# One program block for the opening: feed-forward of batch 0 ahead of the query-weight folding, output weights folded by pairs among the down tiles

## The chip, the cores and the metric

The kernel runs on one core of one Trainium2 chip. The time is the device time of one execution in microseconds (us). The engines are named PE (TensorE), DVE (VectorE), ACT (ScalarE), POOL (GpSimd) and SP (SyncE); ACT and SP also issue the DMA transfers.

## The reference

Four batches of 512 rows of 512 numbers pass a half-weighted feed-forward, a latent attention with 32 heads, and the feed-forward again. All of it is float32.

```python
x = x + 0.5 * ffn(layernorm(x))
x = x + attn(layernorm(x))
x = x + 0.5 * ffn(layernorm(x))

# ffn: W_base 512x512, four active LoRA experts of rank 8, gates from a softmax
y = x @ W_base.T + b_base
alpha = softmax(log(prior + EPS) + x @ router_W.T + router_b)
return y + einsum(lora_B @ (lora_A @ x) * 2, alpha)

# attn
c_q, c_kv, k_rope = x @ w_q_down, x @ w_kv_down, rope(x @ w_k_rope)
q_lat = einsum(c_q @ w_q_up_nope, w_uk)          # w_q_up_nope (192 x 4096), w_uk (4096 x 64)
q_rope = rope(c_q @ w_q_up_rope)
probs = softmax(causal((q_lat . c_kv + q_rope . k_rope) / sqrt(192)))
out = einsum(probs @ c_kv, w_uv) @ w_out          # w_uv (4096 x 64), w_out (4096 x 512)
```

## The kernel before

The weights are prepared once, then the four batches run one after the other. A weight that multiplies in float32 precision is kept as a high part (written by ACT) and a low part (the rest, written by DVE or POOL).

The first program block prepares weights. PE transposes W_base (`wb_hi`, `wb_lo`). It then folds w_uk into w_q_up_nope in eight groups of four heads: `transpose_nope` turns a group into two banks, ACT and DVE copy them out, and `fold_query` multiplies them with `uk_sb`. Behind the first two groups ACT and DVE also split the rotary weights (`rotary_hi`, `rotary_lo`). Last come the LoRA weights, the gate's prior and the down weights (`wd_hi` on ACT, `wd_lo` on POOL). All engines meet at the end of this block.

The second block starts with `steps(-1, FIRST, STEPS)` for batch 0. Its tiles 4 to 7 are the feed-forward of the four row tiles and its tiles 8 to 11 the down projections. For each tile PE does a first half of the products, a transpose for the tile before (`transpose_z` or `transpose_down`), the transpose of the next tile's normalised rows (`transpose_x`), one `fold_output`, the second half, and for a feed-forward tile the LoRA product of the tile before (`lora`). In the opening the tiles alternate over two pairs of PSUM banks, so a tile's first half waits until `update_rows` on DVE has emptied the pair two tiles before. `fold_output` folds w_uv into w_out, four heads at a time, from two staging buffers that SP fills (`load_out`); a buffer is loaded again when PE has used it. POOL computes rough inverse deviations, which DVE refines. After tile 11 come the first query products of batch 0, and then the attention loop.

Each engine runs its own instructions strictly in the written order; semaphores tie the engines together. SP's and ACT's transfers go to one queue each, served in order.

## Time and profile before

| | us |
|---|---|
| median of 3 runs | 1360.4 (1359.52 to 1362.66) |
| the profiled execution, its own time | 1361.4 |
| its span, first to last instruction | 1359.5 |
| PE busy | 1212.1 (89%) |
| DVE busy | 851.1 (63%) |
| ACT busy | 629.7 (46%) |
| POOL busy | 512.1 (38%) |

The busy shares are means over the whole span, of which nine tenths are attention and later feed-forwards that the change doesn't touch. What the change moves lies in the first 128.5 us, so the rows further down are from there. In a timeline row the first number is the start, the second the length from the first to the last of the merged instructions, and the bracket gives idle time ahead of it and who ended it.

### The profile page before, as it was taken

The page shows a single profiled execution, that of the slowest core. Times are in us where ns is not written, and L with a number is a line of the kernel's source. Part 1 is how long each engine was busy: PE and PEld are TensorE (multiplying, and loading weights), DVE is VectorE, ACT ScalarE, POOL GpSimd, SP SyncE. Part 2 cuts the span into 40 slices and gives each one's busy share as a digit, 9 for nine tenths or more (in the row PEclk, how much of TensorE's full clock was granted, in tenths as well). Part 3 has the DMA queues.
Part 4 walks back from the last instruction along what each step waited for, and adds up shares of the span by engine and source line. Part 5 has one row for each costly group of instructions (what it writes and reads, how often), then busy time and mean ns, then how long its engine had stood idle before and what let it go on. Part 6 is the DMA issues. An engine that isn't in the chain of part 4 may idle for free.

```text
span 1359.5 us, 27786 instructions
## 1 busy us (share of the span) xinstructions
PE 1212.1 (89%) x8424; PEld 1014.2 (75%) x8424; DVE 851.1 (63%) x3266; ACT 629.7 (46%) x1810; POOL 512.1 (38%) x821
## 2 busy tenths in 40 slices
PE   3587899999988799999989699999989789999997
PEld 3465788888777678888769578888869678888876
DVE  1564666666667566566667565666666566665655
ACT  1433655555413455555512455555532365555541
POOL 0311544444312344444421254444430254444430
PEclk8799999999989899999989899999998899999998
DMA  9251000000000000000000000000010000000000
GB/s 263 85 169 40 1 1 1 0 0 2 32 24 10 3 2 1 0 0 1 2 32 32 3 1 1 0 0 1 1 32 32 1 1 1 1 0 0 2 1 31
DMA packets 21232, 27.64 MB, mean 20 GB/s; under 512 B 9942, under 2 KB 11734, under 8 KB 20474
## 3 DMA queue, kind: packets, MB, share of 16 engines
q1 hardware_dynamic: 16922, 17.98, 4.2%
q10 hardware_dynamic: 4192, 8.19, 2.1%
q8 instruction: 62, 1.02, 0.3%
q14 instruction: 56, 0.46, 0.1%
HBM read 21.97 MB, written 4.19 MB: 19 GB/s over the span
## 4 chain that ended last, share of the span: by engine, by line
issue 36%; POOL 27%; PE 24%; DVE 6%; ACT 1%; POOLq 1%; DVEq 0%; ACTq 0%
POOL prob L701 20%; POOL q_tok L674 6%; PE Y L747 5%; PE Y L932 4%; PE XZ L747 3%; PE Y L906 3%; PE XZ L891 2%; PE XZ L720 1%; PE Y L793 1%; PE Y L840 1%; DVE x_sb L1301 1%; DVE stats L1106 1%; PE XZ L870 1%; PE Y L852 1%; PE XZ L872 1%
## 5 line engine op out<-in xcount | busy, mean ns | idle before, releaser
L701 POOL TENSOR_TENSOR prob<-prob,small 128x512 f32<-128x512 f32 (+3 forms) x512 | 360.6, 720 | 462.6 <-DVE small L1297 461.7
L1078 ACT ACTIVATE prob<-XZ,small 128x512 f32<-128x512 f32 (+3 forms) x512 | 266.7, 525 | 351.4 <-DVE small L1342 351.3
L1342 DVE CUSTOM_DVE_ANT_0 XZ<-XZ,mask 128x512 f32<-128x512 f32 (+3 forms) x512 | 244.4, 508 | 254.3 <-issue 245.4
L870 PE MATMUL XZ<-kT_hi,qT_hi 128*128 128x512 f32 (+3 forms) x512 | 181.8, 355 | 25.0 <-DVE qT_lo L1290 14.9
L891 PE MATMUL XZ<-ident,prob 128*128 128x128 f32 x1280 | 195.5, 275 | 0.2
L872 PE MATMUL XZ<-kT_hi,qT_lo 128*128 128x512 f32 (+3 forms) x512 | 166.1, 324 | 0.0
L871 PE MATMUL XZ<-kT_lo,qT_hi 128*128 128x512 f32 (+3 forms) x512 | 165.8, 324 | 0.0
L891 PEld LDWEIGHTS XZ<-ident,prob 128*128 128x128 f32 x1280 | 147.5, 140 | 21.1 <-POOL prob L701 7.3
L906 PE MATMUL Y<-probT,ckv 128*64 128x384 f32 (+2 forms) x1280 | 152.3, 384 | 8.6 <-ACT probT L596 8.1
L596 ACT ACTIVATE probT<-XZ 128x512 f32<-128x512 f32 x192 | 114.6, 597 | 79.5 <-PE XZ L891 77.2
L906 PEld LDWEIGHTS Y<-probT,ckv 128*64 128x64 f32 x1280 | 84.1, 136 | 71.2 <-issue 44.0
L674 POOL TENSOR_TENSOR q_tok<-q_tok,q_sin 128x256 f32<-128x256 f32 x128 | 93.2, 728 | 110.3 <-DVE q_sin L1282 105.6
L870 PEld LDWEIGHTS XZ<-kT_hi,qT_hi 128*128 128x128 f32 x512 | 97.3, 190 | 47.8 <-issue 40.7
L1301 DVE TENSOR_TENSOR x_sb<-Y,x_sb 128x512 f32<-128x512 f32 x128 | 87.9, 686 | 70.5 <-PE Y L932 70.2
L932 PE MATMUL Y<-wo_hi,oT_hi 128*128 128x512 f32 (+1 forms) x256 | 111.3, 435 | 1.6 <-DVE x_sb L1301 1.4
L852 PE MATMUL Y<-ident,q_tok 128*128 128x128 f32 x512 | 81.7, 283 | 30.4 <-POOL q_tok L674 30.4
L872 PEld LDWEIGHTS XZ<-kT_hi,qT_lo 128*128 128x128 f32 x512 | 97.2, 190 | 5.8
L932 PE MATMUL Y<-wo_hi,oT_lo 128*128 128x512 f32 (+1 forms) x256 | 100.9, 394 | 0.0
L1078 ACT ACTIVATION_READ_ACCUMULATOR prob<-XZ,small 128x1 f32 x512 | 100.3, 196 | 0.0
L932 PE MATMUL Y<-wo_lo,oT_hi 128*128 128x512 f32 (+1 forms) x256 | 100.0, 391 | 0.0
L871 PEld LDWEIGHTS XZ<-kT_lo,qT_hi 128*128 128x128 f32 x512 | 98.0, 191 | 2.2
L1290 DVE TENSOR_TENSOR qT_lo<-Y,qT_hi 128x512 fp32r<-128x512 f32 x128 | 86.1, 672 | 12.1 <-ACT qT_hi L1047 12.1
(203 smaller groups left out, 2500.3 us busy)
## 6 DMA issues: line engine op xcount, KB each, us to landing
wout_nat<-in_L_attn_w_out_dram SPq DMA_DIRECT2D x8, 1024.0 KB, 5.7
out_dram<-x_sb SPq DMA_DIRECT2D x16, 256.0 KB, 2.0
x_next<-_attn_hidden_states_dram SPq DMA_DIRECT2D x12, 256.0 KB, 2.9
nope_a<-_L_attn_w_q_up_nope_dram ACTq DMA_DIRECT2D x2, 1024.0 KB, 14.5
wbase_nat<-in_L_ffn_W_base_dram ACTq DMA_DIRECT2D x1, 1024.0 KB, 5.5
nope_b<-_L_attn_w_q_up_nope_dram ACTq DMA_DIRECT2D x2, 512.0 KB, 13.3
rope_a<-_L_attn_w_q_up_rope_dram ACTq DMA_DIRECT2D x1, 1024.0 KB, 11.1
rope_bb<-_L_attn_w_q_up_rope_dram ACTq DMA_DIRECT2D x2, 512.0 KB, 13.4
```

The costliest lines, as they stand in the source:

```text
L596: do.activation(probT_unit(v), bank_unit(v), ACT.Copy).then_inc(probT_by_act, 1)
L674: nc.gpsimd.tensor_tensor(rot, rot, q_sin[:, :, ::-1, :], ALU.add).then_inc(q_tok_set, 1)
L701: last = nc.gpsimd.tensor_tensor(prob[u % RING][:, c:c + w], prob[u % RING][:, c:c + w], inv_sum[:, u % RING, m:m + 1].broadcast_to([P, w] ...
L747: last = nc.tensor.matmul(banks_of(s, first(b + 1))[:, half, 0:z - a], xt[s % 2][:, c, :], w[:, c, a:z], start=(c == 0 and j == 0), stop=( ...
L870: nc.tensor.matmul(bank[:, c:c + w], high, kT_hi[:, 0:w], start=True, stop=False)
L871: nc.tensor.matmul(bank[:, c:c + w], high, kT_lo[:, 0:w], start=False, stop=False)
L872: last = nc.tensor.matmul(bank[:, c:c + w], low, kT_hi[:, 0:w], start=False, stop=True)
L891: last = nc.tensor.transpose(probT_ps[v % 2][:, at], prob[v % RING][:, at], ident[:])
L906: last = nc.tensor.matmul(o_ps[64 * h:64 * h + 64, column * P:(column + n) * P], ckv[:, j, :], probT[:, HEAD_BLOCKS * h + at:HEAD_BLOCKS * ...
L932: last = nc.tensor.matmul(bank, o[buffer][:, rows], w, start=(k == 0 and j == 0), stop=(k == 1 and j == 2))
L1078: last = nc.scalar.activation(prob[u % RING][:, c:c + w], score_ps[u % 2][:, c:c + w], ACT.Exp, bias=neg_max[:, u % RING, m:m + 1], scale= ...
L1342: last = nc.vector.tensor_tensor_reduce(bank, bank, mask[:, S - w:S], -1.0, HIGHEST, ALU.add, ALU.min, neg_max[:, u % RING, m:m + 1])
```

## The change

The two program blocks become one, and the opening of every engine is written out by hand.

- ACT issues W_base, then the four row tiles of x (before: SP, behind the small gathers), then w_uk; the first half of w_q_up_nope follows only after the W_base splits. The second half, the rotary weights and the down weights move to SP.
- On SP the LoRA gathers of all four experts go first, the eight small gate gathers (router bias, prior) after them.
- DVE takes the statistics of x among the W_base splits, so tile 4 can be normalised and multiplied before any query weight is folded.
- Order on PE: W_base, tile 4's transpose, LoRA weights, feed-forward tiles 4 to 7, the query folding (with the rotary weights as before), then the down tiles 8 to 11.
- The statistics of the four down tiles are taken together after the last feed-forward tile, and POOL computes their rough deviations in one group, behind `wd_lo`.
- The first two staging buffers of the output weights are loaded without a wait. `fold_output` now takes two heads and one PSUM bank of three (16 folds for 8). Two folds stand ahead of tile 8, then three to a tile, five behind and in tile 11.
- Later batches keep their order; only counts of semaphores change there.

```diff
+        outw_banks = (Y[0][:, 0, :], Y[0][:, 1, :], Z[0])
+        FOLDS_FIRST = (0, 1)
+        FOLDS = {8: ((2,), (3, 4)), 9: ((5,), (6, 7)), 10: ((8,), (9, 10)), 11: ((11,), (12, 13, 14, 15))}
@@ SP: the reload of a staging buffer
-                            sp.wait_ge(outw_ps, g - 1)
+                            sp.wait_ge(outw_ps, 2 * (g - 1))
@@ ACT
+                def opening():
+                    act.dma_start(wbase_nat[:], W_base.rearrange("(c p) h -> p c h", p=P)).then_inc(ffn_in, 16)
+                    for t in range(ST):
+                        act.dma_start(x_sb[:, t, :], hidden[0, t * P:(t + 1) * P, :]).then_inc(x_in[t], 16)
+                    act.dma_start(uk_sb[:], w_uk.rearrange("(h d) r -> d h r", d=DN)).then_inc(uk_in, 16)
+                    for c in range(KC):
+                        base_high(c)
...
@@ POOL
+                    z_constants()
+                    rough_deviations(0, FIRST, ST)
+                    pool.wait_ge(down_hi_set, 1)
+                    nc.gpsimd.tensor_tensor(wd_lo[:], down_nat[:], f32(wd_hi[:]), ALU.subtract).then_inc(down_lo_set, 1)
+                    rough_deviations(1, DOWN, ST)
+                    pool.wait_ge(rope_hi_set, 1)
...
@@ PE
+                def fold_output(i):
+
+                    j, at = (i // 2) % 2, 2 * (i % 2)
+                    pe.wait_ge(out_in[j], 32 * (i // 4 + 1))
+                    if i >= 3:
+                        pe.wait_ge(outw_hi, i - 2)
+                        pe.wait_ge(outw_lo, i - 2)
+                    bank = outw_banks[i % 3]
+                    for h in range(2):
+                        last = nc.tensor.matmul(bank[64 * h:64 * h + 64, :], uv_nat[j][:, at + h, :],
+                                                wout_nat[j][:, at + h, :], start=True, stop=True, tile_position=(0, 64 * h))
+                    last.then_inc(outw_ps, 1)
+                def opening():
+                    transpose_base()
+                    transpose_x(-1, FIRST)
+                    transpose_lora()
+                    pe.wait_ge(lora_lo_set, 1)
+                    for s in range(FIRST, DOWN):
...
+                        ffn_products(-1, s, 0)
...
+                    pe.wait_ge(nope_in[0], 32)
+                    transpose_nope(0, 0)
+                    transpose_z(-1, DOWN - 1)
+                    lora(-1, DOWN - 1)
...
+                    for i in range(G4 // 2):
+                        fold_query(i)
+
+                    transpose_x(-1, DOWN)
+                    for i in FOLDS_FIRST:
+                        fold_output(i)
...
+                        down_products(-1, s, 0)
+                        if s > DOWN:
+                            transpose_down(-1, s - 1)
+                        if s + 1 < STEPS:
+                            transpose_x(-1, s + 1)
+                        for i in FOLDS[s][0]:
+                            fold_output(i)
+                        down_products(-1, s, 1)
+                        for i in FOLDS[s][1]:
+                            fold_output(i)
@@ DVE
+                def opening():
+                    nc.vector.memset(f32(cq_lo[64:P, 1, :]), 0.0)
+                    base_low(0)
+                    base_low(1)
+                    for t in range(ST):
+                        dve.wait_ge(x_in[t], 16)
+                        nc.vector.bn_stats(stats[:, t, :], x_sb[:, t, :]).then_inc(stats_set, 1)
+                    base_low(2)
+                    base_low(3)
...
+                    nopeTb_copy(0, 0)
+                    z_low(-1, DOWN - 1)
+                    update_rows(-1, DOWN - 1)
+                    for s in range(DOWN, STEPS):
+                        dve.wait_ge(x_updated, s - DOWN + 1)
+                        row_stats(-1, s)
+                    dve.wait_ge(stats_set, 2 * ST)
+                    for s in range(DOWN, STEPS):
+                        last = row_moments(s)
+                    last.then_inc(var_set, 1)
+                    deviations(1, DOWN, ST, 2)
+                    norm(-1, DOWN, FIRST)
+                    norm(-1, DOWN + 1, FIRST)
+                    pipelined(dve, query_lo, rotary_lo)
```

The order of instructions shows the change at three places. First, what ACT issues at the program's start, before:

```order
L324 DMA wbase_nat<-in_L_ffn_W_base_dram 128x4x512
L325 DMA uk_sb<-in_L_attn_w_uk_dram 128x32x64
L333 DMA nope_a<-in_L_attn_w_q_up_nope_dram 128x2048
L335 DMA nope_b<-in_L_attn_w_q_up_nope_dram 64x2048
L328 DMA rope_a<-in_L_attn_w_q_up_rope_dram 128x2048
L330 DMA rope_bb<-in_L_attn_w_q_up_rope_dram 64x2048 x2
L333 DMA nope_a<-in_L_attn_w_q_up_nope_dram 128x2048
L335 DMA nope_b<-in_L_attn_w_q_up_nope_dram 64x2048
L341 ACT_TABLE_LOAD
L341 ACTIVATE wb_hi<-XZ 128x256
```

and ACT at the same place of the changed program:

```order
L1004 DMA wbase_nat<-in_L_ffn_W_base_dram 128x4x512
L1006 DMA x_sb<-in_L_attn_hidden_states_dram 128x512 x4
L1007 DMA uk_sb<-in_L_attn_w_uk_dram 128x32x64
L967 ACT_TABLE_LOAD
L967 ACTIVATE wb_hi<-XZ 128x256
```

The first W_base split now stands behind six issues instead of nine, and none of them is a query weight; the two of `nope_a` and `nope_b` that ACT keeps stand behind its eighth activation.

Second, DVE between the last weight work and the first normalised tile of the next stage; before, this is the seam of the two blocks, ahead of the feed-forward:

```order
L501 TENSOR_TENSOR small<-small,router_row 128x4
L278 UNCONDITIONAL_BRANCH
L1094 UNCONDITIONAL_BRANCH
L1110 BN_AGGR moments<-stats 128x2 x4
L1117 TENSOR_TENSOR newton<-rough 128x4
```

and in the changed program the same kind of work stands between the last feed-forward tile and the query folding (`nopeT_b` is the first operand copy of a query group that PE waits for):

```order
L1205 SCALAR_TENSOR_TENSOR x_sb<-XZ,x_sb 128x512
L1134 BN_STATS stats<-x_sb 128x6 x4
L1138 BN_AGGR moments<-stats 128x2 x4
L1145 TENSOR_TENSOR newton<-rough 128x4
L1147 TENSOR_TENSOR newton<-newton,var_eps 128x4
L1149 TENSOR_SCALAR newton<-newton 128x4
L1151 TENSOR_TENSOR rstd<-newton,rough 128x4
L1157 TENSOR_SCALAR xn_79<-x_sb,moments,rstd 128x512
L1157 TENSOR_SCALAR xn_80<-x_sb,moments,rstd 128x512
L1252 COPY nopeT_b_75<-XZ 128x256
L1262 TENSOR_TENSOR wq_lo<-Y,wq_hi 128x4x64
L1265 TENSOR_TENSOR wq_56<-Y,wq_56 64x4x64
```

The copy for the second query group is now queued behind the statistics, the deviations and two normalised tiles.

Third, PE in the third down tile (tile 10), from the transpose of the tile before it to the end of its second half; before:

```order
L782 MATMUL XZ<-ident,down_101 128x128 x3
L720 MATMUL XZ<-ident,xn_89 128x128 x4
L793 MATMUL Y<-wout_nat_128,uv_nat_126 64x512 x4
L756 MATMUL Y<-wd_hi,xT_hi_90 128x320
L756 MATMUL Y<-wd_lo,xT_hi_90 128x320
L756 MATMUL Y<-wd_hi,xT_lo_92 128x320
L756 MATMUL Y<-wd_hi,xT_hi_90 128x320
L756 MATMUL Y<-wd_lo,xT_hi_90 128x320
L756 MATMUL Y<-wd_hi,xT_lo_92 128x320
```

and in the changed program:

```order
L617 MATMUL XZ<-ident,down_92 128x128 x3
L561 MATMUL XZ<-ident,xn_80 128x128 x4
L687 MATMUL XZ<-wout_nat_128,uv_nat_126 64x512 x2
L591 MATMUL Y<-wd_hi,xT_hi_81 128x320
L591 MATMUL Y<-wd_lo,xT_hi_81 128x320
L591 MATMUL Y<-wd_hi,xT_lo_83 128x320
L591 MATMUL Y<-wd_hi,xT_hi_81 128x320
L591 MATMUL Y<-wd_lo,xT_hi_81 128x320
L591 MATMUL Y<-wd_hi,xT_lo_83 128x320
L687 MATMUL Y<-wout_nat_128,uv_nat_126 64x512 x2
L687 MATMUL Y<-wout_nat_129,uv_nat_127 64x512 x2
```

A tile held one fold of four heads; it now holds three folds of two, and the third needs the other staging buffer.

## Rows read from the trace of the kernel before

**Rows 1.** Stretches: length, busy PE, PEld, DVE, ACT, POOL (counts), clock, DMA share, GB/s

```profile
0.00:51.00 51.00, 25.31 (x339) 21.30 (x340) 15.06 (x32) 16.59 (x35) 8.64 (x14) 0.87 0.66 185
51.00:64.90 13.90, 2.03 (x13) 1.31 (x11) 8.92 (x25) 5.35 (x9) 5.63 (x9) 0.61 0.44 123
64.90:118.80 53.90, 46.58 (x266) 31.77 (x267) 29.28 (x78) 18.27 (x43) 6.75 (x28) 0.94 0.47 144
```

**Rows 2.** Timeline of PE: W_base, first query groups, first feed-forward product

```profile
6.42 1.08 PE L393 MATMUL XZ<-ident,wbase_nat 128*128 128x128 f32 x4 [6.42 <-DMA wbase_nat<-in_L_ffn_W_base_dram]
...
28.03 0.48 PE L423 MATMUL XZ<-uk_sb,nopeT_a 128*64 128x64 f32 x4 [7.34 <-ACT nopeT_a L359]
...
31.60 0.48 PE L423 MATMUL Y<-uk_sb,nopeT_a 128*64 128x64 f32 x4
...
40.73 0.48 PE L423 MATMUL Y<-uk_sb,nopeT_a 128*64 128x64 f32 x4 [4.11 <-issue]
...
64.88 0.58 PE L747 MATMUL Y<-wb_hi,xT_hi 128*128 128x292 f32 x1 [1.50 <-DVE xT_lo L1136]
```

**Rows 3.** Timeline of ACT: a blocked issue and the first W_base split

```profile
2.35 6.65 ACTq L333 DMA_DIRECT2D nope_a<-_L_attn_w_q_up_nope_dram  x1
...
14.25 0.38 ACT L341 ACTIVATE wb_hi<-XZ 128x256 fp32r<-128x256 f32 x1
```

**Rows 4.** Timeline of DVE: W_base's last split, statistics, moments, first normalised tile, row update

```profile
18.86 0.41 DVE L455 TENSOR_TENSOR wb_lo<-Y,wb_hi 128x256 fp32r<-128x256 f32 x1
...
52.99 2.47 DVE L491 BATCH_NORM_STATS2 stats<-x_sb 128x6 f32<-128x512 f32 x4
...
58.64 0.38 DVE L1110 BATCH_NORM_AGGREGATE moments<-stats 128x2 f32<-128x6 f32 x4 [1.17 <-PEq L278]
...
61.47 1.19 DVE L1129 TENSOR_SCALAR xn<-x_sb,moments,rstd 128x512 f32<-128x512 f32 x2
...
85.49 0.68 DVE L1177 SCALAR_TENSOR_TENSOR x_sb<-XZ,x_sb 128x512 f32<-128x512 f32 x1
```

**Rows 5.** DMA queues from 12 to 16 us (q10 ACT's, q1 SP's): packets, MB

```profile
q10 hardware_dynamic: 176, 1.30, 98.8%
q1 hardware_dynamic: 172, 0.02, 3.9%
```

**Rows 6.** Timeline of PE: an output fold, and the first halves of tiles 5 to 7

```profile
68.38 1.94 PE L793 MATMUL Y<-wout_nat,uv_nat 128*64 128x512 f32 x8
...
71.77 0.30 PE L747 MATMUL XZ<-wb_hi,xT_hi 128*128 128x292 f32 x1
...
78.95 0.40 PE L747 MATMUL Y<-wb_hi,xT_hi 128*128 128x292 f32 x1 [0.89 <-DVE x_sb L1177]
...
86.23 0.41 PE L747 MATMUL XZ<-wb_hi,xT_hi 128*128 128x292 f32 x1 [0.89 <-DVE x_sb L1177]
```

**Rows 7.** Timeline of PE in tiles 9 to 11: two waits, a fold, one half tile

```profile
100.58 0.41 PE L756 MATMUL XZ<-wd_hi,xT_hi 128*128 128x320 f32 x1 [1.96 <-DVE x_sb L1177]
...
102.90 3.09 PE L793 MATMUL Y<-wout_nat,uv_nat 128*64 128x512 f32 x8
...
112.07 0.41 PE L756 MATMUL Y<-wd_hi,xT_hi 128*128 128x320 f32 x1
...
113.05 0.31 PE L756 MATMUL XZ<-wd_hi,xT_hi 128*128 128x320 f32 x1
...
115.44 0.55 PE L782 MATMUL Y<-ident,down 128*128 128x128 f32 x3 [1.35 <-ACT ckv L1000]
```

**Rows 8.** SP's issue of the third output load; landing of all eight

```profile
71.09 0.38 SPq L625 DMA_DIRECT2D wout_nat<-in_L_attn_w_out_dram  x1
...
DMA to landing us min/median/max: 5.0/5.7/7.9
```

**Rows 9.** Timeline of PE: first query products and first scores

```profile
118.76 0.28 PE L840 MATMUL Y<-wq_hi,cq_hi 128*128 128x256 f32 x1
...
128.54 0.47 PE L870 MATMUL XZ<-kT_hi,qT_hi 128*128 128x512 f32 x1 [1.50 <-DVE qT_lo L1290]
```

More of the change, by code:

```diff
@@ L260, in rounds, with pipelined @@
                 body(i)
-        def pipelined(eng, opening, body, between):
-            opening()
+        def pipelined(eng, body, between):
             body(0)
@@ L683, in steps @@
                     z_constants()
-                    if start == 0:
-                        rough_deviations(group + (2 if end > FIRST else 1), 2, 2)
+                    rough_deviations(group + (2 if end > FIRST else 1), 2, 2)
                     if end > DOWN:
@@ L797, in steps, with transpose_base @@
-                def steps(b, start, end):
-                    transpose_x(b, start)
-                    for s in range(start, end):
+                def transpose_base():
+                    pe.wait_ge(ident_set, 3)
+                    pe.wait_ge(ffn_in, 16)
+                    for c in range(KC):
+                        if c >= 2:
+                            pe.wait_ge(base_hi, c - 1)
+                            pe.wait_ge(base_lo, c - 1)
+                        for o in range(KC):
+                            last = nc.tensor.transpose(weights_ps[c % 2][:, o * P:(o + 1) * P],
+                                                       wbase_nat[:, o, c * P:(c + 1) * P], ident[:])
+                        last.then_inc(baseT_ps, 1)
@@ new lines, in transpose_lora @@
+                def transpose_lora():
+                    pe.wait_ge(lora_in, 16 * (3 * NE + 1))
+                    pe.wait_ge(base_lo, KC)
+                    for c in range(KC):
+                        last = nc.tensor.transpose(weights_ps[1][:, c * (NZ + NE):(c + 1) * (NZ + NE)],
+                                                   lora_nat[:, c * P:(c + 1) * P], ident[0:NZ + NE, 0:NZ + NE])
+                    last.then_inc(loraT_ps, 1)
+                    pe.wait_ge(up_filled, 1)
+                    for o in range(KC):
+                        last = nc.tensor.transpose(weights_ps[0][:, o * P:(o + 1) * P], up_nat[:, o, :], ident[:])
+                    last.then_inc(upT_ps, 1)
@@ new lines, in transpose_nope @@
+                def transpose_nope(g, j):
+                    for h in range(4):
+                        nc.tensor.transpose(nopeTa_ps[j][:, h * P:(h + 1) * P],
+                                            nope_a[:, 4 * g + h, :], ident[:])
+                    for h in range(4):
+                        last = nc.tensor.transpose(nopeTb_ps[j][:, h * 64:(h + 1) * 64],
+                                                   nope_b[:, 4 * g + h, :],
+                                                   ident[0:64, 0:64])
+                    last.then_inc(nopeT_ps, 1)
@@ L801, in steps @@
+                def steps(b, end):
+                    transpose_x(b, 0)
+                    for s in range(end):
                         products = ffn_products if s < DOWN else down_products
-                        wait_for_products(b, s, start)
+                        wait_for_products(b, s)
                         products(b, s, 0)
-                        if s > start:
+                        if s:
                             (transpose_z if s <= DOWN else transpose_down)(b, s - 1)
@@ L1018, in steps @@
+                def steps(b, end):
+                    xT_high(b, 0)
+                    for s in range(end):
+                        if s:
                             (z_high if s <= DOWN else ckT_high)(b, s - 1)
@@ new lines, in steps @@
+                def steps(b, end):
+                    group, roughs = 2 + 3 * b, GROUPS_0 + GROUPS * b
+                    norm(b, 0)
+                    norm(b, 1)
+                    dve.wait_ge(y_added, 32 * (b + 1))
+                    for t in (2, 3):
+                        row_stats(b, t)
+                    xT_low(b, 0, 12 * b + 8 + (2 * ST if end > FIRST else ST))
+                    row_moments(2)
+                    row_moments(3).then_inc(var_set, 1)
+                    if end > FIRST:
+                        deviations(group + 1, FIRST, ST, roughs + 1)
+                        deviations(group + 2, 2, 2, roughs + 3)
+                    else:
+                        deviations(group + 1, 2, 2, roughs + 2)
+                    for s in range(end):
+                        if 0 <= s - 2 < DOWN:
```

675 lines of the change are left out of this document (343 added, 332 removed).

## The prediction

> **What bounds the kernel now.** I read the page first: PE is busy in 89% of the span, but that mean says nothing of the opening. So I split the first 128.5 us by what PE works on [rows 1]. The reader is to see four stretches. The first 51 us prepare weights, with PE busy for 25.3 of them. Then come 13.9 us in which PE is busy for 2.03: the last weights, the seam of the two blocks, and the norm of the first tile. The feed-forward, the down tiles and the output folds take 53.9 us with PE busy for 46.6. The first queries take 9.8 (118.76 to 128.54) [rows 9]. Everything after 128.5 us keeps its order, so what the change is worth is the start of batch 0's scores, 128.54 us now [rows 9], against where they start afterwards.
>
> Next the timelines of each engine, to see who is late. Three things hold up the first stretch. ACT's DMA issue of `nope_a` blocks for 6.65 us, so the first W_base split starts at 14.25 [rows 3] although the transposes it needs ran from 6.42 to 7.50 [rows 2]. The query folding starts at 28.03 after PE waited 7.34 us. And it stops for 4.11 us in the middle, for the rotary weights [rows 2]. During all this x isn't used at all. The third stretch is close to PE's own work, so there the sum is one of PE time plus waits.
>
> **The change part by part.** I write the new opening as a chain on the clock of the profile.
>
> *Start to first product.* Nothing blocks ACT any more, so the splits start at 7.5. From their start to the last low part took 5.0 us (14.25 to 19.27) [rows 3, 4]. The statistics of x, 2.47 us [rows 4], are put between; W_base's 1 MB had landed at 6.42 [rows 2], so x, the next MB on the same queue, should be there near 10.2 (estimate), and part of the 2.47 fits in DVE's gaps. I take 14.1 for the end. From moments to the first norm is 2.83 us (58.64 to 61.47) [rows 4], from there to the first product 3.41 (61.47 to 64.88) [rows 2, 4]: 20.3. The LoRA gathers may be later than that. In 12 to 16 us the two queues moved 172 and 176 packets [rows 5], one for one, so SP's small packets pass at the rate of ACT's large ones while `nope_a` and `nope_b` stream, here 1.5 MB or some 5 us. I add 0.9: first product at 21.2. The gate's own gathers come last, but the gate is used only behind the first half tile, and I count nothing for them; if that cover were gone, it would be the same few us as in the rival below.
>
> *Feed-forward.* The first half of tile 4 runs at 64.88, of tile 5 at 71.77, of 6 at 78.95, of 7 at 86.23 [rows 2, 6]. Each period holds one output fold of 1.94 us that now moves away: 4.95, 5.24 and 5.34 remain. The waits of 0.89 us for `update_rows` stay, since DVE's 0.68 us starts right when PE's LoRA product ends [rows 4, 6]. In the first period DVE's low part of the next tile loses its cover, which was the fold; I add 0.35. Tile 7's first half then starts at 37.1. What is left of it (two halves, one LoRA product, without another transpose) I take as 3.7, and 2.9 for the first query transposes, the wait for DVE and the last LoRA product: 43.7. These two are estimates, the periods above less the transpose and the wait.
>
> *The new wait.* Here a stall comes back. DVE's copy for the second query group is queued behind the last row update, four statistics, moments to norm, and two norms: 0.68 + 2.47 + 2.83 + 1.19 [rows 4], with the copy itself of about 0.4 and starts 7.7. PE can do one group of folding, then it waits some 4.5 us. The second group starts at 51.4. POOL's `wd_lo` runs beside DVE's statistics, ends about with them and costs nothing more; if it were late, each us would be one of the total. From the second group to the end took 19.2 us (31.60 to 50.8) [rows 1, 2], with its stop for the rotary weights and a slow clock at its start, and both come again: 70.7. The seam of the blocks itself is gone, and 13.9 us have become these 4.5.
>
> *Down tiles and output folds.* One transpose and two folds: 2.5, so tile 8 starts at 73.2. PE's work from there is eight half tiles of 0.98 (112.07 to 113.05) [rows 7], fourteen folds of 0.95, a little under half of 1.94 [rows 6], and the transposes, for which I take 2.7 together (estimate): 23.8 us. Now the loads. A buffer is free when a pair of folds has ended, and from the end of a fold to the landing is 0.77 us until the issue (70.32 to 71.09) and 5.0 to 5.7 of transfer [rows 6, 8]; 6.1 together. With two folds and the two buffers loaded ahead, the chain is: fold 1 ends at 73.2, fold 4 can start at 79.3; 4.5 us of work bring fold 5 to its end, fold 8 can start 6.1 after that; 2.9 us bring fold 9 to its end, fold 12 can start 6.1 after that; then fold 11's own reload holds fold 14, and two folds follow. That is 30.9 us from tile 8 to the last fold, 7.1 more than PE's work: 104.1. What is late is always the load, since the folds of 1.1 MB used to be 7.3 us apart and now are nearer.
>
> *First queries.* 9.8 us as before [rows 9], of which I take 0.3 off, because the last down tile's copies are done long before: 113.6.
>
> *Clock.* After 1.96 us of idle, the longest in the down tiles, the fold took 3.09 us [rows 7] for 1.94, as at 1.2 GHz; after the three of 0.89 and the two of 1.35 it stayed fast (two and one of them stand in [rows 6, 7]). The new waits are of 1 to 2.4 us. I count one such fall, 0.45 on the transpose and 1.15 on the fold: 1.6, so 115.2.
>
> The sum: 128.5 less 115.2 is 13.3 us. The profiled execution took 1361.4 with its span of 1359.5, which gives 1348.1; it lies 1 us above the median of 1360.4, and against that the forecast is 1347.1.
>
> A rule speaks against this change more than my one fall does. The Trainium skill, TensorE: Matmul & The Clock Gate, section "HAM oscillation — how this bites in real kernels", says that a kernel whose short bursts of matmuls alternate with DMA waits starts every burst at the low clock. The trace shows one fall in six such waits, after 1.96 us and not after 0.89 or 1.35, so I hold to one.
>
> **The rivals.**
>
> *Every load wait drops the clock.* Four waits at 1.6 us each is 6.4 for the 1.6 in the sum: 1351.9. For it speaks the fall after 1.96 us, against it that no shorter wait did it. The rule just named gives this time.
>
> *The loads are slower.* Two are in flight at once, and the pair that was issued together took up to 7.9 us [rows 8]. That is 2.6 more in three rounds: 7.8, so 1354.9. For it speaks that new loads follow each other every 5 us; against it that 1.1 MB in 5 us is 220 GB/s, while the stretch moved 144 with pauses [rows 1].
>
> *The loads hide.* If a reload lands while PE does other things, because the tiles before are slower than I think, the 7.1 and the 1.6 fall away: 1338.4.
>
> *The small gathers are late.* If SP's packets go one for one behind large ones throughout [rows 5], the first product comes 5 us later: 1352.1. Against it: ACT's queue holds only half of `nope` then.
>
> *Slower than before.* PE's clock stays at 1.2 GHz from the wait at 45 us to the scores. A query group took 3.57 us at that level (28.03 to 31.60) [rows 2] and 19.2 for seven is 2.7 on average, so 6 us more; the down stretch at 3.09 for 1.94 [rows 6, 7] is 14 more of which the load waits absorb about 3. With 17 us lost it is 1364. It decides from 13.3 us lost, that is, a low clock for some three quarters of 51 to 104 us. Against it, 0.94 was granted in the whole third stretch, with PE busy for 86% of it [rows 1]; after, it is 75 to 80%.
>
> **How the numbers follow.** The forecast with its own spread (1343 to 1351) has 0.50. Each load wait dropping the clock 0.10, slower loads 0.10, late gathers 0.10, hidden loads 0.13; slower than before 0.03. The other 0.04 is that waits which I haven't seen eat most of it. The range goes from the hidden loads to the slower loads, 1338 to 1355.5, and leaves about 0.12 out. A measurement here tells apart 0.2%, 2.7 us. All cases but the last two gain more: faster 0.94, same 0.03, slower 0.03.
>
> **What would show it.** In the new profile: the first W_base split near 7.5; the first feed-forward product near 21; three periods near 5.3 with DVE ending a wait of 0.9 in each; a wait of PE of 4 to 5 us for DVE's `nopeT_b` before the second query group, near 51; the folding's end near 71; waits of 1 to 2.4 us ahead of folds 4, 8, 12 and 14; the first scores at 113 to 116; and from there to the end the same 1231 us. The forecast is wrong if SP's gathers hold up DVE ahead of the first low part, if `wd_lo` on POOL ends after DVE's moments, or if the granted clock is low in the down tiles.

## The result, and the profile after

The changed kernel takes 1347.7 us (median of 4 runs, 1345.4 to 1348.5) where the kernel before, run beside it, took 1361.5. The ratio is 0.990, with a 95% interval of 0.988 to 0.992: 1.0% faster. The profiled execution has a span of 1346.4 us.

First the windows of PE's stretches, as in [rows 1], cut where the changed program changes its work (columns as there). They are: weights, feed-forward, query folding, down tiles, first queries.

```profile
0.00:19.20 19.20, 6.61 (x28) 4.93 (x28) 8.96 (x29) 4.94 (x12) 4.77 (x21) 1.00 0.88 253
19.20:42.30 23.10, 20.07 (x136) 19.08 (x137) 11.37 (x40) 8.95 (x21) 0.00 (x0) 1.00 0.98 276
42.30:68.90 26.60, 19.25 (x315) 16.46 (x313) 16.00 (x37) 12.24 (x24) 10.75 (x4) 0.81 0.06 22
68.90:105.50 36.60, 29.43 (x138) 13.56 (x137) 18.43 (x45) 15.74 (x39) 0.00 (x0) 0.95 0.62 194
105.50:115.20 9.70, 4.84 (x33) 3.78 (x31) 5.12 (x15) 3.01 (x7) 1.45 (x2) 0.88 0.00 0
```

The reader is to see where PE rests: 12.6 us of the first 19.2, then 3.0 in the feed-forward, 7.4 in the folding and 7.2 in the down tiles. The scores start at 115.24 for 128.54 [rows 9], and from there to the end it is 1231.2 us for 1231.0. So the gain of the profiled execution, 13.3 us, lies wholly in the first part.

The timeline of PE gives the stations of that chain and the waits ahead of them (its other waits are left out):

```profile
19.20 0.61 PE L582 MATMUL Y<-wb_hi,xT_hi 128*128 128x292 f32 x1
...
20.10 0.45 PE L582 MATMUL Y<-wb_hi,xT_hi 128*128 128x292 f32 x1
...
25.63 0.38 PE L582 MATMUL XZ<-wb_hi,xT_hi 128*128 128x292 f32 x1 [0.43 <-DVE xT_lo L1164]
...
30.70 0.40 PE L582 MATMUL Y<-wb_hi,xT_hi 128*128 128x292 f32 x1 [0.78 <-DVE x_sb L1205]
...
35.81 0.41 PE L582 MATMUL XZ<-wb_hi,xT_hi 128*128 128x292 f32 x1 [0.80 <-DVE x_sb L1205]
...
49.71 0.48 PE L670 MATMUL Y<-uk_sb,nopeT_a 128*64 128x64 f32 x4 [4.32 <-DVE nopeT_b L1252]
...
68.86 0.66 PE L561 MATMUL XZ<-ident,xn 128*128 128x128 f32 x4
...
71.40 0.38 PE L591 MATMUL Y<-wd_hi,xT_hi 128*128 128x320 f32 x1
...
77.69 1.08 PE L687 MATMUL Y<-wout_nat,uv_nat 128*64 128x512 f32 x4 [1.65 <-DMA wout_nat<-in_L_attn_w_out_dram]
...
88.67 1.08 PE L687 MATMUL XZ<-wout_nat,uv_nat 128*64 128x512 f32 x4 [0.88 <-DMA wout_nat<-in_L_attn_w_out_dram]
...
92.73 1.08 PE L687 MATMUL Y<-wout_nat,uv_nat 128*64 128x512 f32 x4 [0.90 <-DMA wout_nat<-in_L_attn_w_out_dram]
...
99.38 3.58 PE L687 MATMUL Y<-wout_nat,uv_nat 128*64 128x512 f32 x8 [2.08 <-DMA wout_nat<-in_L_attn_w_out_dram]
...
103.65 1.08 PE L687 MATMUL XZ<-wout_nat,uv_nat 128*64 128x512 f32 x4 [0.69 <-DMA wout_nat<-in_L_attn_w_out_dram]
...
115.24 0.76 PE L825 MATMUL XZ<-kT_hi,qT_hi 128*128 128x512 f32 x1 [1.50 <-DVE qT_lo L1425]
```

The two waits that the change adds stand in it: 4.32 us for DVE's `nopeT_b` ahead of the second query group, and five waits for `wout` of 6.20 us together, behind the longest of which the two folds took 3.58 us for 1.94. One more wait is no part of the forecast. The first one for `xT_lo`, 0.43 us, has the gate behind it, as the timeline of DVE shows:

```profile
21.92 0.17 DVE L1309 TENSOR_SCALAR prior_raw<-prior_raw 128x4 f32<-128x4 f32 x1 [1.37 <-DMA prior_raw<-_L_ffn_domain_prior_dram]
...
24.07 0.16 DVE L1178 RECIPROCAL small<-small 128x1 f32<-128x1 f32 x1 [1.12 <-ACT small L946]
...
24.81 0.68 DVE L1164 TENSOR_TENSOR xT_lo<-XZ,xT_hi 128x512 fp32r<-128x512 f32 x1
```

Tile 5's `xT_lo` is queued behind the gate of tile 4, and that behind the last small gathers; on ACT a table load of 1.28 us stands between. It would be more than 0.43, had tile 4 not been slow itself, as e10 below bears out: its first twelve products start 0.24 us apart, and later ones 0.135.

### The profile page after: what moved, and what is told of

Read it like the earlier page. It is cut to its first block, busy times and chain, and to the rows that moved or that the text cites. A ratio compares the mean times of both kernels' runs of the same rounds, so it can differ in the third digit from the quotient of the medians.

```text
span 1346.4 us, 27795 instructions
## 1 busy us (share of the span) xinstructions
PE 1214.1 (90%) x8424; PEld 1014.5 (75%) x8424; DVE 852.1 (63%) x3278; ACT 632.3 (47%) x1818; POOL 507.8 (38%) x795
## 4 chain that ended last, share of the span: by engine, by line
issue 37%; POOL 28%; PE 24%; DVE 6%; DMA 2%; ACT 1%; POOLq 1%; SPq 1%; ACTq 0%; DVEq 0%
POOL prob L542 21%; POOL q_tok L491 6%; PE Y L582 4%; PE Y L887 4%; PE XZ L582 4%; PE Y L861 2%; PE XZ L846 2%; DMA wout_nat<-in_L_attn_w_out_dram 1%; PE XZ L561 1%; PE Y L795 1%; DVE stats L1134 1%; DVE x_sb L1436 1%; PE XZ L825 1%; PE Y L807 1%; PE XZ L827 1%
## 5 line engine op out<-in xcount | busy, mean ns | idle before, releaser
L807 PE MATMUL Y<-ident,q_tok 128*128 128x128 f32 x512 | 81.9, 283 | 30.9 <-POOL q_tok L491 30.9
```

## The experiments

The theory is that the time is that of the chain above, each wait costing its length. Its rivals are that a wait which is taken away comes back on another engine, and that the clock decides instead. The table has, for each kernel, its median and the profiled execution's stations in us: the first product, tile 5, the length of the folding (second nope transposes to tile 8's transpose), of the down tiles (first down product to first query product), and the start of the scores. The rest, from there to the end, was 1229.6 to 1232.7 us in all of them.

| kernel | median | first product | tile 5 | folding | down tiles | scores |
|---|---|---|---|---|---|---|
| changed | 1347.7 | 19.20 | 25.63 | 26.52 | 34.12 | 115.24 |
| e1_loads_once | 1342.2 | 19.28 | 26.77 | 27.17 | 25.55 | 108.58 |
| e2_spread_stats | 1347.0 | 19.35 | 26.96 | 25.20 | 32.23 | 113.03 |
| e3_gate_early | 1346.2 | 19.20 | 24.97 | 26.51 | 30.74 | 111.28 |
| e4_nope_early | 1351.5 | 25.20 | 30.64 | 26.69 | 31.36 | 118.31 |
| e5_three_buffers | 1339.4 | 19.44 | 25.65 | 26.67 | 25.53 | 106.98 |
| e6_rotary_spread | 1345.3 | 19.30 | 26.97 | 22.02 | 32.48 | 110.13 |
| e7_all | 1335.4 | 19.46 | 25.44 | 21.44 | 25.65 | 102.08 |
| e8_all_warm | 1335.4 | 18.87 | 24.62 | 21.04 | 25.74 | 100.52 |
| e9_rotary_late | 1333.3 | 19.30 | 25.09 | 18.02 | 27.48 | 104.67 |
| e10_late_warm | 1331.7 | 18.86 | 24.93 | 15.84 | 27.27 | 97.70 |
| e11_pool_late | 1330.9 | 19.41 | 25.19 | 16.44 | 25.95 | 97.53 |
| e12_best | 1328.4 | 18.84 | 22.92 | 16.44 | 25.78 | 94.55 |

Runs of one kernel differ by 1.5 to 7 us, so a step of 1 us is read from the stations, not from the median.

**e1_loads_once**, the output weights loaded for four pairs only.

```diff
-                    rounds(sp, G4 // 2, load_out)
+                    load_out(0)
-                    pe.wait_ge(out_in[j], 32 * (i // 4 + 1))
+                    pe.wait_ge(out_in[j], 32)
```

> The changed kernel, but uv and wout are loaded for the first four head pairs only, and the folds 4 to 15 use those again, so w_out's part of the other pairs is left out of the output. Theory A (the reloads bound the down tiles): the five DMA waits of PE ahead of folds 4, 8, 10, 12 and 14, 1.65, 0.88, 0.90, 2.08 and 0.69 us, together 6.2, and the slow fold of 12 and 13 (3.58 for 1.94, so 1.6) go away: the scores start at 107.4 for 115.2, and the time is 7.8 us less, 1339.9. Rival B (ACT and DVE, which copy each fold and each down tile, are nearly as late as the loads): half of the waits come back as waits for wo_hi, wo_lo or ckT_lo, and it is 3 to 4 us. Rival C (the clock falls anyway, since PE then rests less but still often): 6.2 only.

The down tiles took 25.55 us for 34.12: A, and 0.8 us more than it gave. No wait came back; the two that are left are for `xn`, 1.0 us together, and the changed kernel has them too. The scores come only 6.7 us earlier, since in this profile the gate was later (tile 5 at 26.77) and the folding 0.65 us longer, which the edit doesn't touch. The medians differ by 5.5 us, less than A's 7.8; the runs of each kernel are 3.0 and 4.7 us apart, and the changed kernel's profiled execution is the slowest of its four.

**e2_spread_stats**, the down tiles' statistics put among the query groups on DVE.

```diff
-                    for s in range(DOWN, STEPS):
-                        dve.wait_ge(x_updated, s - DOWN + 1)
-                        row_stats(-1, s)
...
-                    pipelined(dve, query_lo, rotary_lo)
+                    for g in range(G4):
+                        query_lo_group(g)
+                        if g < 2:
+                            for s in (DOWN + 2 * g, DOWN + 2 * g + 1):
...
+                                row_stats(-1, s)
```

> The changed kernel with the statistics, moments, deviations and norms of the down tiles taken from ahead of DVE's second query group and put behind its first four: two statistics behind each of the first two groups, the moments behind the second, the deviations behind the third, the two norms behind the fourth. Theory A (the wait costs its length, and the rest fits under PE): PE's 4.32 us of idle ahead of the second group go, and the folding ends 4.3 us earlier, or about 6 if the clock then stays at its high level in the groups that run at the low one now. 1343.4 to 1341.7. Rival B (DVE has no room among the groups): the 5.1 us of statistics and norms come back among the groups as waits for nopeT_b or wq_lo, and the time stays within 1 us of 1347.7. Rival C (the stop for the rotary weights on ACT and DVE, 52.3 to 58.3 us now, is what ends last): it only moves forward with the groups if the rotary weights have landed; then A holds, else the gain is under 1 us.

The wait of 4.32 us went, and the folding got only 1.3 us shorter. The timeline of PE in this kernel has what took its place:

```profile
54.95 0.34 PE L670 MATMUL Y<-uk_sb,nopeT_a 128*64 128x64 f32 x4 [3.62 <-issue]
...
59.97 0.48 PE L670 MATMUL Y<-uk_sb,nopeT_a 128*64 128x64 f32 x4 [1.59 <-ACT nopeT_a L977]
```

The first is the stop for the rotary weights, 2.70 us in the changed kernel. The second row names ACT's copy, which was done at 59.02; what came last was DVE's copy of the same group, from 59.45 to 59.87. DVE had been held by an operation on 128 x 4 elements, which takes 0.16 us elsewhere. The timelines of DVE and, below it, of POOL:

```profile
55.78 3.04 DVE L1145 TENSOR_TENSOR newton<-rough 128x4 f32<-128x4 f32 x1
...
59.45 0.42 DVE L1252 COPY nopeT_b<-Y 128x256 f32<-128x256 f32 x1
```

```profile
52.95 5.85 POOL L514 TENSOR_TENSOR wq_lo<-rope_a,wq_hi 128x2048 fp32r<-128x2048 f32 x1
```

DVE's operation ended at 58.82, when POOL's rotary low part did, 58.80. The median fell by 0.7 us. So B and C were both partly right: the wait is real, but the stop for the rotary weights stood behind it, and the deviations in their new place met POOL, which they don't in the changed kernel.

**e3_gate_early**, router bias and prior read from fixed rows ahead of the LoRA gathers.

```diff
+                    sp.dma_start(prior_raw[:], domain_prior[0:NE].unsqueeze(0).broadcast_to([P, NE])).then_inc(gate_in, 16)
+                    sp.dma_start(router_row[:], router_b[0:NE].unsqueeze(0).broadcast_to([P, NE])).then_inc(gate_in, 16)
...
-                    dve.wait_ge(gate_in, 16 * 2 * NE)
+                    dve.wait_ge(gate_in, 32)
```

> The changed kernel, but the router bias and the prior of the gate are read from the first four experts' rows in two DMAs ahead of everything that depends on the active list, in place of eight gathers by that list behind those of the LoRA weights, so the gate's constants may belong to other experts than the reference's. Theory A (the gate's gathers are late, but their lateness is nearly covered): DVE's wait of 1.37 us for prior_raw goes, ACT is done with the gate of tile 4 a good us earlier, and PE's 0.43 us of idle ahead of tile 5 goes; 0.4 us less, 1347.3, not to be told from no change. Rival B (the chain behind them holds up every tile of the feed-forward): 1.4 us or more less. Rival C (two issues ahead of the LoRA gathers make those late): up to 1 us more.

Tile 5 came at 24.97 with no wait ahead of it, 0.66 us earlier: A. But against e1, e2 and e6, where the gate's waits were 1.5 to 1.7 us, it is 1.8 to 2.0. DVE takes up the gathered prior at 21.92 us in the changed kernel and at 23.05 to 23.26 in those three, so when the gathers land differs by over 1 us from run to run. The down tiles, which the edit doesn't touch, were 3.4 us shorter than in the changed kernel, with 4.6 us of DMA waits for 6.2 and no slow fold: that much the loads and the clock vary too.

**e4_nope_early**, the order of ACT's DMAs undone.

```diff
+                    act.dma_start(nope_a[:, 0:16, :], w_q_up_nope[0:P, 0:16 * DN]
+                                  .rearrange("q (h d) -> q h d", d=DN)).then_inc(nope_in[0], 16)
...
                     for c in range(KC):
                         base_high(c)
```

> The changed kernel with the one edit of ACT's queue undone: the first halves of nope_a and nope_b are issued ahead of the W_base splits, as in the kernel before. Theory A (what lets the feed-forward begin at 19.2 us is that no DMA issue blocks ACT any more): the issue of nope_a blocks again, for some 6.7 us, the first split comes at 14 for 7.4 us, the first product at 26, and the time is 6.7 us more, 1354.4. Rival B (x and the norm, 15.9 us, or the LoRA gathers hold the first product anyway): part of it is covered; the statistics can run ahead of nothing, since they stand behind two low parts on DVE, so at most the 0.7 us of PE's and ACT's slack is: 6.0. Rival C (the issue does not block, since uk and the rest are small): no change.

The issue blocked again, as the timeline of ACT shows:

```profile
4.55 7.10 ACTq L1008 DMA_DIRECT2D nope_a<-_L_attn_w_q_up_nope_dram  x1
```

PE waited 6.75 us between W_base's transposes, and the first product came at 25.20, 6.0 us later, as Rival B had it. At tile 5 it was 5.0, since the gate's gathers had landed meanwhile. The median rose by 3.8 us. So this one order is worth 4 to 6 of the 13.3 us.

**e5_three_buffers**, a third staging buffer in the space that the small weights leave.

```diff
+        wout_nat.append(place("wout_nat2", [P, 4, D], F32, third))
+        uv_nat.append(place("uv_nat2", [P, 4, KVL], F32, third))
...
-                            sp.wait_ge(outw_ps, 2 * (g - 1))
+                        if g > 2:
+                            sp.wait_ge(outw_ps, 2 * (g - 2))
```

> The changed kernel with a third staging buffer for uv and wout, loaded once wd_lo is done (45.5 us), so six head pairs' weights lie ready when the down tiles begin, and a reload has the time of four folds instead of two. Theory A (the five waits are the latency of one load behind the last use of its buffer): the down tiles, from tile 8's first product to the first query product, take what they take without reloads, 25.6 us for 34.1, so 8.5 us less, 1339.2. Rival B (what bounds is the DMA engines' rate with two loads in flight: 1.1 MB in 5 us is 220 GB/s, and five loads are left from 71.6 us on): the last lands at 96.6 us at the earliest, the first query product comes at 98.6, and it is 28 us for 25.6: 6 to 7 us less than now, 1341.5. Rival C (two loads in flight land later each, up to 7.9 us): waits of 1 us stay in some rounds, 4 us less.

25.53 us, what it takes without reloads, and 8.3 us less in the median. The view of PE's waits in these 25.5 us shows that no product waits for a load:

```profile
PE XZ L568 <- DVE xn L1164: 1.0, 2, 0.5
```

A holds. 220 GB/s was not the limit that Rival B took it for: from 82 to 87 us the DMA engines moved 286, as the view of windows shows (columns as in [rows 1]).

```profile
82.00:87.00 5.00, 4.53 (x25) 2.13 (x21) 3.23 (x11) 2.85 (x8) 0.00 (x0) 1.00 0.98 286
```

**e6_rotary_spread**, DVE's and ACT's splits of `rope_bb` in quarters, ACT's copy of `rope_a` ahead of tile 7's gate, and POOL's low part behind the norms. Shown is ACT's quarter.

```diff
+                def rotary_b_hi(k):
+                    act.wait_ge(rope_in, 32)
+                    h = slice(8 * k, 8 * k + 8)
+                    nc.scalar.activation(wq2[:, h, KVL:HD], rope_bb[:, h, :], ACT.Copy).then_inc(rope_b_hi, 1)
...
+                        if 2 <= g < 6:
+                            rotary_b_hi(g - 2)
```

> The changed kernel with its stop for the rotary weights taken apart: ACT's copy of rope_a (1.91 us) goes ahead of tile 7's gate, rope_bb's goes in four quarters behind query groups 2 to 5, DVE's low part of it (2.29 us) in four quarters behind groups 3 to 6, and POOL takes the low part of rope_a only once both norms of the down tiles are done. Theory A (ACT's 3.8 us in a row, 52.3 to 55.9, and DVE's 2.29 behind them are what PE waits 2.70 us for, and PE's sequencer another 1.7): both go, and some of the low clock behind them; the folding from the second nope transposes to its end takes 22 us for 26.5, so 4 to 5 us less, 1343. Rival B (the waits go elsewhere: each quarter of about 0.6 us lands on ACT, 1.36 of 2.06 us busy in a group, and on DVE, 1.25 of 2.06): ACT's share is then 1.9 of 2.06 us and PE waits for it in each of four groups, 2 us less in all. Rival C (what holds the folding is the low clock behind DVE's 4.3 us wait): the groups stay at the low level and it is under 1 us.

The folding took 22.02 us: A, with the wait of 4.3 us still in it. The median fell by 2.4 us, not by A's 4 to 5, and the scores came 5.1 us earlier; in this profile tile 5 was 1.3 us late and the down tiles 1.6 us short, which the edit doesn't touch.

**e7_all**, the edits of e5 and e6, the statistics in the feed-forward's gaps, and the prior's gathers first.

```diff
+                        if s - 2 >= FIRST:
+                            down_stats(s + 2)
                         gate_logits(-1, s)
...
+                        if g == 0:
+                            deviations(1, DOWN, ST, 2)
+                        if g == 1:
+                            norm(-1, DOWN, FIRST)
```

> The changed kernel with every wait that was found taken out of PE's way: three staging buffers; the rotary weights in quarters; the statistics of the down tiles taken on DVE in the feed-forward's gaps, the deviations behind the first query group and the norms behind the second; POOL does wd_lo and the rotary low part behind these; the gate's prior is gathered ahead of the router bias, with a wait of its own. Theory A (these waits are all that stands between the changed kernel and PE's work): tile 5 at 25.0, the second nope transposes at 41.7, eight groups of 2.06 us, so tile 8 at 61, the down tiles in 26 to 28 us and the scores some 9.7 later, at 97 to 99 for 115.2: 1330 to 1332. Rival B (the loads: the third buffer's load now starts at 54 and the reloads at 62, two in flight for 25 us): the down tiles take 31 and it is 1335. Rival C (DVE or ACT are the bound once the groups take 2.06 us): 2.5 us a group, 1335 as well, with waits for wq_lo or nopeT_b in most groups.

The down tiles held, the folding did not: 21.44 us for the 16.5 of eight groups. PE stood 3.82 us until 57.52, behind a copy of DVE's that ran from 56.99 to 57.41, and the timelines of DVE and, below it, of POOL show why:

```profile
52.18 4.80 DVE L1269 TENSOR_TENSOR wq<-rope_bb,wq 64x512 fp32r<-64x512 f32 x1
...
58.24 0.68 DVE L1269 TENSOR_TENSOR wq<-rope_bb,wq 64x512 fp32r<-64x512 f32 x1
```

```profile
51.91 4.52 POOL L525 TENSOR_TENSOR wq_lo<-rope_a,wq_hi 128x2048 fp32r<-128x2048 f32 x1
```

The same operation took 4.80 us beside POOL's and 0.68 without it. The median is the 1335 of Rivals B and C, but for a reason that neither names.

**e11_pool_late** adds one wait to e7, so that POOL's rotary low part starts behind DVE's last quarter; **e9_rotary_late** moves DVE's quarters to the down tiles instead.

```diff
                     pool.wait_ge(rope_hi_set, 1)
+                    pool.wait_ge(rope_b_lo, 4)
```

> The kernel of run e7 with one wait added on POOL: its rotary low part starts when DVE's four quarters are done, so neither is moved among PE's groups, and only the overlap of the two goes. Theory A (as for e9: the 4.80 us quarter waited for POOL): each quarter takes 0.68 us and the folding takes 17 to 18 us for 21.4; POOL starts near 58 and ends by 65, ahead of the first queries that read it, so 4 us less than e7, 1331.4. Rival B (the quarter was late for another reason, such as the split of rope_bb on ACT or its landing): the 4.8 us quarter stays, and so does the time.

> The kernel of run e7 with one thing moved: DVE's four quarters of the rotary low part go from behind query groups 3 to 6 to among the down tiles, where POOL is done. In e7 one such quarter, 64 x 512 elements, took 4.80 us on DVE where the others took 0.68, from 52.18 to 56.98, while POOL did its rotary low part from 51.91 to 56.43, and PE waited 3.8 us for the copy behind it. Theory A (DVE and POOL can't both work from SBUF at once, and the quarter waited for POOL): without it the groups take 2.06 us throughout, the folding takes 17 us for 21.4, the low clock behind the wait goes too, and it is 4.5 us less than e7, 1331. Rival B (ACT's copies are the bound in the groups with a rotary quarter, whatever DVE does): 1 us less. Rival C (the quarters hold up the down tiles on DVE in their new place, 0.68 us each): 2 us less.

In e11 all four quarters took 0.68 us and the folding 16.44: A, shown. The timelines of DVE (the last quarter) and, below it, of POOL:

```profile
58.23 0.68 DVE L1270 TENSOR_TENSOR wq<-rope_bb,wq 64x512 fp32r<-64x512 f32 x1
```

```profile
59.05 4.56 POOL L526 TENSOR_TENSOR wq_lo<-rope_a,wq_hi 128x2048 fp32r<-128x2048 f32 x1 [7.25 <-DVE wq L1270]
```

Nobody waited for POOL there. Against the changed kernel the folding is 10.1 us shorter. 6.5 of these are idle time of PE, and 3.6 are its busy time, 15.58 us for 19.17, at a granted clock of 1.00 for 0.81 in that stretch: here the waits cost their length and what the low clock added behind them.

e9 shortened the folding too, to 18.02, but its quarters held up `xn` in the down tiles (waits of 1.30 and 1.38 us for 0.5), as its Rival C had it, and its own profile had one more wait: ACT, which stood at `rope_a`'s landing, was late with `zT_hi`, and PE waited 2.69 us. (That execution took 1338.5 us, the slowest of the four.)

**e8_all_warm** and **e10_late_warm** add to e7 and e9 24 transposes that nobody reads, in PE's idle time ahead of the first norm.

```diff
                     transpose_base()
+                    for _ in range(24):
+                        nc.tensor.transpose(Y[0][:, 0, 0:P], ident[:], ident[:])
```

> The kernel of the run before with 24 transposes of the identity into an unused bank in PE's idle 5.6 us ahead of the first norm, which is work that nobody reads. Theory A (tile 4's products run at the low clock, 0.24 us from one to the next for 0.135 later, because PE idled ahead of them): 18 such steps and the transposes are faster, 2 us, and since the gate now comes early enough, most of it, 1.5 us, is won. Rival B (the gate's chain on DVE and ACT holds tile 5 as soon as tile 4 is fast): the gain turns into a wait for xT_lo, and it is 0.5 us or less. Rival C (the clock does not rise for such work): no change.

> The kernel of run e9 with the 24 unread transposes of run e8 ahead of the first norm. Theory A (they raise the clock for the first tile's products; in e8 tile 5 came at 24.6 us for 25.4): 0.8 to 1.6 us less than e9, if what follows keeps its length. Rival B (the gate's gathers, which end DVE's wait at 22 us, differ from run to run by a us, and cover it): no difference that can be told.

In e8 tile 5 came 0.8 us earlier than in e7 and the median stayed; e10's was 1.6 us below e9's, whose spread is 6.8. The timeline of PE in e10 says more:

```profile
10.80 4.20 PE L715 MATMUL Y<-ident 128*128 128x128 f32 x24
...
16.57 0.66 PE L572 MATMUL XZ<-ident,xn 128*128 128x128 f32 x4 [1.57 <-DVE xn L1179]
...
18.86 0.40 PE L593 MATMUL Y<-wb_hi,xT_hi 128*128 128x292 f32 x1 [0.67 <-DVE wb_lo L1329]
19.10 0.29 PE L593 MATMUL Y<-wb_lo,xT_hi 128*128 128x292 f32 x1
19.23 0.30 PE L593 MATMUL Y<-wb_hi,xT_lo 128*128 128x292 f32 x1
...
24.93 0.38 PE L593 MATMUL XZ<-wb_hi,xT_hi 128*128 128x292 f32 x1 [2.34 <-DVE xT_lo L1186]
```

Tile 4's products were 0.13 us apart from the second on. From its first product to its last it took 3.45 us for 5.67 in e9, and the 2.2 us saved became a wait of 2.34 us for the gate's chain. The order on DVE and ACT was a hidden bound. In e8 the same transposes helped less: three steps of some 0.15 us, then 0.24 again up to 21.34 us.

**e12_best** takes that away too: both copies of tile 5's transposed x stand ahead of tile 4's gate, `rope_a` is split in quarters, and the rest is e11's with the 24 transposes.

```diff
                     nc.scalar.activation(prior_row, prior_raw[:], ACT.Ln).then_inc(prior_ln, 1)
+                    xT_high(-1, FIRST + 1)
```

> The kernel of run e11 with the 24 unread transposes of runs e8 and e10, with rope_a's split on ACT in quarters behind query groups 0, 1, 6 and 7 (it held up tile 6's LoRA product by 2.69 us in e9, where the weights landed late), and with both copies of tile 5's transposed x ahead of the gate of tile 4. In e10 tile 5's first product came at 24.93 us, 2.34 us after PE had finished tile 4, and e11's at 25.19. Theory A (what holds tile 5 is the order on ACT and DVE, where x's copies are queued behind the gate and so behind its gathers and a table load of 1.28 us): the first product of tile 5 comes at 22.8 us, the scores at 95.2 for e11's 97.5, and the time is 2.3 us less than e11, 1328.6. Rival B (the gate itself is needed for tile 5's LoRA product, so the wait only moves from the first product to the transpose of z or to x_sb): 1 us or less. Rival C (the quarters on ACT behind groups 0 and 1 hold up groups of 2.06 us): it takes back 0.5 to 1 us.

Tile 5 came at 22.92 us, as A had it, and tile 6 kept 1.8 of the 2.3; the scores came at 94.55 for A's 95.2. The time is 1328.4 us (median of 5 runs, 1326.9 to 1332.6), 0.976 of the kernel before with an interval of 0.974 to 0.977. It beats both kernels.

## Why the prediction was right, and which terms were off

The forecast of the time was 1347.1 for 1347.7, and the scores came at 115.24 for 115.2. The mechanism was right in the main: the feed-forward ahead of the folding, the new wait, and the loads as the bound of the down tiles. That the numbers meet so closely is luck. Tile 8 came 1.8 us earlier than forecast (71.40 for 73.2), and the down tiles took 1.6 us longer (34.12 for 32.5); other kernels with the same down tiles took 30.7 to 32.5.

- *Start to first product*, 21.2: it was 19.20. The norm started at 15.86 for 16.9, since DVE was done with W_base at 13.36 for 14.1, and the 0.9 us for late LoRA gathers wasn't needed: `fill_up` ran at 16.78 without a wait.
- *Feed-forward*. The periods of 5.24 and 5.34 were 5.07 and 5.11. The first, 4.95 and 0.35, was 6.43. Two things were missing in it: PE starts tile 4 at the low speed, and the gate. "I count nothing for them", said of the gate's gathers, was the step that failed: e10 shows 2.34 us behind that cover once the tile is fast, and in e1, e2 and e6 1.5 to 1.7 showed even without.
- *The new wait*, 4.5: it was 4.32, and the second group started at 49.71 for 51.4, 1.7 us early as the stations before it were. The 19.2 us from there were 19.15. That the wait costs its length is only half true, as e2 shows: the stop for the rotary weights stood right behind it, and the moved deviations met POOL.
- *Down tiles*: 30.9 and 1.6 were forecast, 34.12 it was. PE's work was mis-sized: 23.8 us in the sum, 25.5 in e1 and e5, where no load is waited for; 1.0 of that is the two waits for `xn`, which the sum had left out. The load waits were 7.1 in the sum and 6.20 in the profile, and e1 and e5 show that they bound. A fifth wait, 0.90 us ahead of fold 10, was not foreseen. That they come as a chain of latency held, but the round of 6.1 us, from the end of a buffer's last fold to the next use, was too short: it was 6.3, 6.4, 7.5, 7.5 and 7.4 for the five folds that waited. The six loads of `wout` took 5.2 to 6.7 us from issue to landing, 6.1 in the middle, where the sum had 5.0 to 5.7.
- *Clock*, 1.6: the two folds after 2.08 us took 3.58 for 1.94, at a granted clock of 0.54. One fall in the five load waits, as forecast. But four more kernels run the same down tiles. e2 and e6 had one fall each, behind waits of 1.78 and 2.36 us; e3 and e4 had none, with 1.00 granted throughout. The timelines of PE in e4 and, below it, in e6 show the folds behind their longest waits:

```profile
103.21 1.94 PE L687 MATMUL Y<-wout_nat,uv_nat 128*64 128x512 f32 x8 [2.20 <-DMA wout_nat<-in_L_attn_w_out_dram]
```

```profile
95.43 3.30 PE L689 MATMUL Y<-wout_nat,uv_nat 128*64 128x512 f32 x8 [2.36 <-DMA wout_nat<-in_L_attn_w_out_dram]
```

  No fall followed 2.20 us and one followed 1.78, so the length of a wait alone doesn't decide it. The down tiles took 32.2 to 34.1 us in the three kernels with a fall and 30.7 and 31.4 without, and the one fall of the sum came in those three only. What else decides it stays open.
- *First queries*, 9.5: 9.72. The rest, 1231 as before: 1231.2.

Of the rivals, "every load wait drops the clock" did not come: four of the five waits left the clock where it was. The prediction set the Trainium skill, TensorE: Matmul & The Clock Gate, section "HAM oscillation — how this bites in real kernels", beside this rival; the kernel described there waits longer for its DMA than PE did in any of the five, so these runs don't speak against the page, and the rule did not apply to these waits. "The loads are slower" came in part, with 6.7 us for the slowest and not 7.9. "The loads hide" is what e5 brings about. "The small gathers are late" did not come for the first product, at 19.20; the gate's gathers were late, and cost 0.43 us here.

## What to carry to other kernels

Write the opening as a chain on the clock and ask at each step what is queued behind a wait on its engine. A wait that is as long as it looks can still hide two others behind it, so take one away and read the same stretch again. Where a buffer's reload is the latency of one load behind its last use, a third buffer can take the waits away (8.3 us here). And keep a long operation of POOL apart from DVE's operations with two inputs in SBUF.

## What the runs showed of the hardware

DVE and POOL held each other up for whole instructions. DVE's 64 x 512 quarter took 4.80 us in e7 and ended 0.55 us behind POOL's operation; 128 x 4 elements took 3.04 in e2; both have two inputs in SBUF. In the changed kernel DVE was there first, took its 2.29 us, and POOL's operation took 6.63 for 4.52. The timelines of DVE and, below it, of POOL:

```profile
56.01 2.29 DVE L1248 TENSOR_TENSOR wq<-rope_bb,wq 64x2048 fp32r<-64x2048 f32 x1 [2.73 <-ACT wq_hi L973]
```

```profile
56.06 6.63 POOL L514 TENSOR_TENSOR wq_lo<-rope_a,wq_hi 128x2048 fp32r<-128x2048 f32 x1 [8.66 <-ACT wq_hi L973]
```

DVE's copies out of PSUM, 0.42 us, ran beside it undisturbed, and so did its four statistics, which read one tile in SBUF, beside `wd_lo` (2.46 us, as without POOL). The Trainium skill, SBUF — State Buffer, section "SBUF: two separate sides", says that the port pair which the two share is an exclusive lock for a whole instruction, for whichever starts first; of DVE's operations it names those with two SBUF inputs (against a POOL operation that reads SBUF) and those in a two-port mode. These numbers agree. One pair doesn't show it: in e2 DVE's 2.29 us operation began at 52.12, within a POOL operation on 128 x 4 elements from 51.97 to 52.98, and was not held.

The granted clock of a window doesn't show every slow start. In the window from 19.4 to 22.3 us tile 4's products go 0.24 us apart, for 0.135 later, in the changed kernel and, but for the first of them, in e8. The view of windows gives 1.00 for the changed kernel and, below it, 0.50 for e8:

```profile
19.40:22.30 2.90, 2.90 (x13) 2.88 (x14) 0.86 (x2) 1.88 (x3) 0.00 (x0) 1.00 0.54 146
```

```profile
19.40:22.30 2.90, 2.90 (x16) 2.88 (x14) 0.61 (x4) 1.91 (x3) 0.00 (x0) 0.50 0.78 200
```

In e10, after 4.2 us of transposes, they went 0.13 apart from the second on; in e8, after 3.6 us of them, only the first few did. Why the two differ is not shown. Behind the wait of 4.32 us in the changed kernel the granted clock does show the slow groups, 0.50 from 49.7 to 53 us, where the level is 1.2 GHz:

```profile
49.70:53.00 3.30, 3.29 (x39) 2.85 (x40) 1.62 (x5) 1.27 (x3) 0.00 (x0) 0.50 0.02 5
```

ACT loaded a table for Ln at 19.85 us and another for Exp at 22.35, 1.28 us each.
